# Long cross-attention by pairs of heads: scores of two heads on 64-row groups of TensorE, keys made per pair

## The reference

```python
q_hk = (hidden_q @ Wq.T).reshape(Bv, Sv, H, K)             # 256 queries, 16 heads of 128
q_big = jnp.einsum('bshk,hkq->bshq', q_hk, w_kc_q)         # 384 per head
q_big = _apply_rope(q_big, ...)
kv_r = _apply_rope(kv_c, ...)                              # 4096 x 128, one for all heads
q_r = jnp.einsum('bshq,hqr->bhsr', q_big, W_qr)            # rank 64
k_r = jnp.einsum('bld,hdr->bhlr', kv_r, W_kr)              # rank 64, per head
scores = jnp.einsum('bhsr,bhlr->bhsl', q_r, k_r)
attn = jax.nn.softmax(scores, axis=-1)
ctx_c = jnp.einsum('bhsl,bld->bhsd', attn, kv_r)
ctx_lat = jnp.einsum('bhsd,hkd->bhsk', ctx_c, w_kc_kv)
return ctx_lat.transpose(...).reshape(...) @ Wo.T          # layer ffn: |w| row max / 127, round, clip
```

## Time and profile before

| | us |
|---|---|
| median of 3 runs (range) | 1131.75 (1131.22 to 1132.66) |
| the profiled execution: its time | 1130.86 |
| its span, first to last instruction | 1129.2 |

### The profile page before, as it was taken

The page is one execution under the profiler, slowest core; times in us unless marked ns, Lnnn a source line. Parts: engine busy times, 40 slices in busy tenths (PEclk is TensorE's granted clock), DMA queues, the critical chain, the costliest instruction groups (busy, mean ns, idle before and its releaser), DMA issues.

```text
span 1129.2 us, 19389 instructions
## 1 busy us (share of the span) xinstructions
PE 1066.1 (94%) x6663; PEld 862.3 (76%) x6663; DVE 760.1 (67%) x1314; ACT 544.7 (48%) x1075; POOL 334.2 (30%) x232
## 2 busy tenths in 40 slices
PE   7989999999998998999999999999999999899995
PEld 5545889999976665888888888888898889677742
DVE  3656466556636666878888878888877887464545
ACT  3344354454423221666556566666566667343422
POOL 6810243444333000023333213333311333404411
PEclk9999899999999999999999999999999999999998
DMA  9450167655503334112111232212222211223010
GB/s 281 94 222 1 42 225 256 219 201 216 182 25 118 109 103 163 59 30 41 32 35 17 40 40 40 35 35 29 23 40 40 40 31 40 24 76 154 1 61 19
DMA packets 70510, 97.07 MB, mean 86 GB/s; under 512 B 35361, under 2 KB 52929, under 8 KB 69314
## 3 DMA queue, kind: packets, MB, share of 16 engines
q1 hardware_dynamic: 70466, 96.50, 30.2%
HBM read 91.58 MB, written 4.90 MB: 85 GB/s over the span
## 4 chain that ended last, share of the span: by engine, by line
PE 73%; DVE 17%; issue 5%; ACT 3%; DMA 1%; POOL 1%; DVEq 0%; SPq 0%; ACTq 0%; POOLq 0%
PE PS L1362 11%; PE PS L1471 11%; PE PS L1491 10%; PE PS L1481 7%; PE PS L1381 5%; DVE qsL L1024 3%; DVE pL L1050 3%; DVE scores L1030 3%; PE PS L1420 2%; PE PS L1439 2%; PE PS L1429 2%; PE PS L1210 2%; PE PS L1549 2%; PE PS L1508 1%; PE PS L1632 1%
## 5 line engine op out<-in xcount | busy, mean ns | idle before, releaser
L1030 DVE TENSOR_SCALAR_CACHE_REDUCE scores<-PS 128x512 f32<-128x512 f32 x256 | 173.9, 689 | 87.8 <-PE PS L1471 87.0
L750 ACT ACTIVATE scores<-scores,nmX 128x512 f32<-128x512 f32 x256 | 181.9, 714 | 52.8 <-DVE nmX L1034 52.4
L768 ACT ACTIVATE pH<-PS 128x1024 fp32r<-128x1024 f32 x128 | 131.0, 1023 | 152.9 <-PE PS L1481 152.9
L550 POOL TENSOR_TENSOR wrow<-wrow,winv 88x1024 f32<-88x1024 f32 x16 | 30.3, 1892 | 466.8 <-DVE winv L1070 466.8
L1050 DVE TENSOR_TENSOR pL<-PS,pH 128x1024 fp32r<-128x1024 f32 x128 | 156.2, 1220 | 7.5 <-ACT pH L768 7.5
L1481 PE MATMUL PS<-ident,scores 128*128 128x128 f32 x1024 | 136.4, 274 | 17.9 <-ACT scores L750 16.1
L1481 PEld LDWEIGHTS PS<-ident,scores 128*128 128x128 f32 x1024 | 115.9, 141 | 44.5 <-issue 34.0
L1491 PE MATMUL PS<-pH,kvH 128*128 128x256 f32 x512 | 146.5, 286 | 0.3
L1491 PE MATMUL PS<-pH,kvL 128*128 128x256 f32 x512 | 144.7, 283 | 0.0
L1491 PE MATMUL PS<-pL,kvH 128*128 128x256 f32 x512 | 144.4, 282 | 0.0
L1471 PE MATMUL PS<-kvTH,qsH 128*128 128x512 f32 x256 | 111.2, 434 | 2.0 <-DVE qsL L1024 1.5
(11 more groups left out here) (305 smaller groups left out, 2298.0 us busy)
## 6 DMA issues: line engine op xcount, KB each, us to landing
rawG<-in_wg SPq DMA_DIRECT2D x16, 768.0 KB, 5.7
rawU<-in_wu SPq DMA_DIRECT2D x16, 768.0 KB, 7.2
rawD<-in_wd SPq DMA_DIRECT2D x16, 768.0 KB, 6.3
wrow<-in_w SPq DMA_DIRECT2D x16, 352.0 KB
win<-in_win SPq DMA_DIRECT2D x1, 4640.0 KB, 17.5
wblk<-blocks SPq DMA_DIRECT2D x4, 1056.0 KB, 8.1
wb<-w_rows SPq DMA_DIRECT2D x32, 128.0 KB, 3.3
wqX<-in_wqX SPq DMA_DIRECT2D x16, 256.0 KB, 2.6
```

The lines of the kernel that those rows point to most:

```text
L750: act.activation(at, at, ACT.Exp, bias=nmX[:, b, q:q + 1], accum_out=csum[:, b, q, c:c + 1]).then_inc(exp_done, 1)
L768: act.activation(pH[:, c % 2], PS[:, 2 + 2 * (c % 2):4 + 2 * (c % 2), :].rearrange("p k (h t) -> p (k h) t", t=T), ACT.Copy).then_inc(pH_r ...
L1030: dve.tensor_scalar(sp_[:, q, c * CH:(c + 1) * CH], PS[:, q, :], 1.0, None, ALU.mult, ALU.max, accum_out=cmax[:, q, c:c + 1]).then_inc(sX_ ...
```

## The change

Heads go in pairs p; 16 slots s (or j) per pair take the place of 8 chunks per head.

- `p4` is gone. Instead `keys(p, c)` makes the keys of both heads of a pair, 64 rows for the one and 64 for the other: three matmuls 128x512 for each of 8 chunks of each pair, into bank 7; ACT copies `keyH`, DVE makes `keyL`.
- `scores(p, s)` makes chunk s // 2 and query half s % 2 for both heads: three steps of two matmuls, on rows 0 to 63 for head 0 (bank 0), on rows 64 to 127 for head 1 (bank 1). It waits until both heads' banks of the slot before are evicted (`sX_out`, 2 per slot).
- `turn(p, j)` and `weigh(p, j)` do head j % 2, chunk j // 2.
- `p3(m)` makes two heads' ranks in one group, side by side in 64-column groups.
- DVE evicts head 0's scores, makes `pL`, evicts head 1's scores; then `add_out`, `low_keys` or `row_max`.
- `qsL` and the new `wkrL` move from DVE to POOL. `keyH`, `keyL` lie where `kvr` lay, so ACT waits for `kvL_ready` ahead of the first `qh`.
- Weight rows go in 15 jobs of 256 or 128 whole rows in place of 16 of 120; `load_rows` of a job waits for `wint_ready` of the job before, and DVE's first `row_max` of it for `wrow_in`. The last layer's strided patterns become plain ones; `win` is loaded during the last pair. The loops are written out.

```diff
+            for p in range(XP):
+                sp.wait_ge(wint_ready, 2 * p + 1)
+                if p + 1 < XP:
+                    load_rows(2 * p + 1)
+                store_rows(2 * p)
...
+                if p:
+                    sp.wait_ge(oX_ps, 4 * p)
+                    load_out(p)
+                if p + 1 < XP:
+                    sp.wait_ge(wint_ready, 2 * p + 2)
+                    load_rows(2 * p + 2)
+                    store_rows(2 * p + 1)
...
+            def low_parts(p):
+                pool.wait_ge(wkrH_ready, p + 1)
+                pool.tensor_tensor(wkrL[:, p % 2], wkr[:, p % 2], wkrH[:, p % 2].bitcast(F32), ALU.subtract).then_inc(wkrL_ready, 1)
+                pool.wait_ge(qsH_ready, p + 1)
+                pool.tensor_tensor(qsL[:, p % 2], qr[:, p], qsH[:, p % 2].bitcast(F32), ALU.subtract).then_inc(qsL_ready, 1)
...
+            for p in range(2):
+                low_parts(p)
+            pool.wait_ge(qr_ready, XP)
+            for n in range(JOBS):
+                round_rows(n)
+                if n % 2 == 0 and n // 2 + 2 < XP:
+                    low_parts(n // 2 + 2)
...
+            high_parts(0)
+            high_parts(1)
+            act.wait_ge(kvL_ready, 1)
...
+            def scores_out(p, s, heads=range(2)):
+
+                c, q = s // 2, s % 2
+                dve.wait_ge(sX_ps, p * SLOTS + s + 1)
+                for h in heads:
+                    dve.tensor_scalar(sp_[:, h, q, c * CH:(c + 1) * CH], PS[:, h, :], 1.0, None, ALU.mult, ALU.max,
+                                      accum_out=cmax[:, h, q, c:c + 1]).then_inc(sX_out, 1)
+                    if c == NCH - 1:
+                        dve.wait_ge(sX_out, 2 * (p * SLOTS + s) + h + 1)
...
+            for p in range(XP):
+                for j in range(SLOTS):
+                    if j and p + 1 < XP:
+                        scores_out(p + 1, j - 1, (0,))
+                    dve.wait_ge(pH_ready, SLOTS * p + j + 1)
+                    dve.tensor_tensor(pL[:, j % 2], PS[:, 2 + 2 * (j % 2):4 + 2 * (j % 2), :].rearrange("p k (h t) -> p (k h) t", t=T),
+                                      pH[:, j % 2].bitcast(F32), ALU.subtract).then_inc(pL_ready, 1)
+                    if j and p + 1 < XP:
+                        scores_out(p + 1, j - 1, (1,))
+                    if p and j in (4, 6, 8, 10):
+                        add_out(p - 1, (j - 4) // 4, (j - 4) // 2 % 2, 7)
+                    if j % 2 and j + 1 < SLOTS and p + 1 < XP:
+                        low_keys(p + 1, (j + 1) // 2)
+                    if j == SLOTS - 2 and p + 2 < XP:
+                        low_keys(p + 2, 0)
+                    if p + 1 < XP and j in (0, 2):
+                        row_max(2 * p + 1, j // 2)
+                    if p + 1 < XP and j in (12, 14):
+                        row_max(2 * p + 2, (j - 12) // 2)
+                    if j == SLOTS - 1 and p + 1 < XP:
+                        scores_out(p + 1, SLOTS - 1)
+                dve.wait_ge(exp_done, 2 * SLOTS * (p + 1))
+                dve.tensor_reduce(recX[:, p % 2], csum[:, p % 2], AX.X, ALU.add).then_inc(csum_done, 1)
...
+            def keys(p, c):
+
+                if c == 0:
+                    pe.wait_ge(wkrL_ready, p + 1)
+                for j, (w, v) in enumerate(((wkrH, kvTH), (wkrH, kvTL), (wkrL, kvTH))):
+                    mm = pe.matmul(PS[:, 7, :], w[:, p % 2, :], v[:, c * CH:(c + 1) * CH], start=(j == 0), stop=(j == 2))
+                mm.then_inc(key_ps, 1)
...
+            def scores(p, s):
+
+                c, q = s // 2, s % 2
+                if s == 0:
+                    pe.wait_ge(qsL_ready, p + 1)
+                if q == 0:
+                    pe.wait_ge(keyL_ready, p * NCH + c + 1)
+                wait(pe, sX_out, 2 * (p * SLOTS + s))
+                for j, (w, v) in enumerate(((qsH, keyH), (qsH, keyL), (qsL, keyH))):
+                    for h in range(2):
+                        rank = slice(XR * h, XR * h + XR)
+                        mm = pe.matmul(PS[:, h, :], w[rank, p % 2, q * P:(q + 1) * P], v[rank, c * CH:(c + 1) * CH], start=(j == 0), stop=(j == 2),
+                                       skip_group_check=True)
+                mm.then_inc(sX_ps, 1)
...
+            for p in range(XP):
+                more = p + 1 < XP
+                for j in range(SLOTS):
+                    turn(p, j)
+                    if j and more:
+                        scores(p + 1, j - 1)
+                    if p and j == 2:
...
+                        keys(p + 1, (j + 1) // 2)
+                    if j:
+                        weigh(p, j - 1)
+                    if j == SLOTS - 2 and p + 2 < XP:
+                        pe.wait_ge(keyL_ready, (p + 2) * NCH)
+                        keys(p + 2, 0)
+                    if j == SLOTS - 1 and more:
+                        scores(p + 1, SLOTS - 1)
+                weigh(p, SLOTS - 1)
+            values(XP - 1)
```

More of the change, by code:

```diff
@@ new lines, in _ @@
+            act.wait_ge(kvL_ready, 1)
+            for n in range(XH):
+                act.wait_ge(p1_done, n + 1)
+                wait(act, p2_done, n - 1)
+                act.activation(qh[:, n % 2], PS[:, n % 2, 0:T], ACT.Copy).then_inc(qh_ready, 1)
+                if n % 2 and n >= 5:
+                    ranks_out((n - 5) // 2)
+                    if (n - 5) // 2 < 2:
+                        high_query((n - 5) // 2)
+                if n % 2 == 0 and n:
+                    high_keys(0, n // 2 - 1)
@@ L785, in _ @@
+            contexts_out(XP - 1)
+            values_out(XP - 1)
             for t in range(NT):
@@ L1078, in _, with low_keys @@
-            step(dve.memset(wmax[:], 0.0))
-            for b in range(2):
-                stage_query(b, b)
-            for c in range(NCH):
-                scores_out(0, c, 0)
-            pairs(dve, dve_scores)
-            add_out(XH - 1, 1, 0)
-            add_out(XH - 1, 1, 1)
+                wait(dve, p3_done, (n - 4) // 2 + 1)
+                dve.tensor_tensor(qb[:, n % 4], qm1[:], qm2[:], ALU.add).then_inc(qb_ready, 1)
+            def low_keys(p, c):
+                dve.wait_ge(keyH_ready, p * NCH + c + 1)
+                at = slice(c * CH, (c + 1) * CH)
+                dve.tensor_tensor(keyL[:, at], PS[:, 7, :], keyH[:, at].bitcast(F32), ALU.subtract).then_inc(keyL_ready, 1)
@@ L1528, in _ @@
-            pe.wait_ge(kvL_ready, 1)
-            for c in range(NCH):
-                scores(0, 0, c)
-            turn(0, 0)
-            pairs(pe, pe_scores)
-            values(XH - 1, 1, XH // 2)
-            for q in range(NT):
-                head_out(XH - 1, 1, q)
-            stay_awake(14, 0)
+            for n in range(XH):
+                if n + 1 < XH:
+                    p1(n + 1, (n + 1) // 2, (n + 1) % 2)
+                if n % 2 and n >= 3:
+                    p3((n - 3) // 2)
+                p2(n, n // 2, n % 2)
+                if n % 2:
+                    wait(pe, keyL_ready, n // 2)
+                    keys(0, n // 2)
@@ new lines, in weigh @@
+            def weigh(p, j):
+                h, c = j % 2, j // 2
+                pe.wait_ge(pL_ready, SLOTS * p + j + 1)
+                if c == 0:
+                    wait(pe, cT_ready, p)
+                for m in range(4):
+                    for k, (w, v) in enumerate(((kvH, pH), (kvH, pL), (kvL, pH))):
+                        mm = pe.matmul(PS[:, 6, h * T:(h + 1) * T], w[:, 4 * c + m, :], v[:, j % 2, m, :],
+                                       start=(j == 0 and m == 0 and k == 0), stop=(c == NCH - 1 and m == 3 and k == 2), skip_group_check=True)
+                mm.then_inc(v_done, 1)
@@ new lines, in values, with head_out @@
+            def values(p):
+                pe.wait_ge(wo2_in, (p + 1) * 32)
+                pe.wait_ge(cT_ready, p + 1)
+                for h in range(2):
+                    mm = pe.matmul(PS[:, 7, h * T:(h + 1) * T], kcv[:, h, :], cT[:, h, :], start=True, stop=True)
+                mm.then_inc(vX_ps, 1)
+            def head_out(p, h, q, bank):
+                pe.matmul(PS[:, bank, :], vT[:, h, q * P:(q + 1) * P], woX[:, h, :], start=True, stop=True).then_inc(oX_ps, 1)
+            for s in range(SLOTS):
+                scores(0, s)
+                if s == 1:
+                    wait(pe, keyL_ready, NCH)
+                    keys(1, 0)
```

495 lines of the change are left out of this document (224 added, 271 removed).

## The result

The changed kernel takes 1156.1 us (median of 4 runs, 1151.4 to 1159.5) against 1131.6 for the kernel before: a ratio of 1.0215, 95% interval 1.0183 to 1.0248. It is slower by 24.5 us, inside the forecast's own range (1134 to 1165) and 9.4 above its number. The profiled execution took 1156.57 us, 25.7 more than that of before.

What follows compares the result with a forecast made beforehand. The prediction took PE's sequence to bound the kernel. Projections -13.5, first scores +32.7, seven pairs -22, last pair +21.2 and last layer -3.5 gave +14.9 on 1130.86, a median of 1146.7 us; range 1106 to 1172, forecast's own 1134 to 1165.

Steps and rivals of the forecast that it cites:

- What bounds it, and the slot: PE's sequence bounds the heads; a paired slot takes 3.38 us, 4.08 with keys, including 0.39 for shape changes.
- The first rival: Changes of weight shape in the score slots cost nothing: 1108 us, faster; chance 16%.
- the fourth: Rival: score steps of two heads do not overlap with fp32r, +0.70 on 128 slots, 1236 us; chance 2%.
- the 0.216: PE's time in us per 256 columns of a matmul, taken from L1420's row of the earlier profile.
- The pairs: Seven pairs in the overlapped loop take 473 us against 495.1: -22, with 67.3 per pair.
- The row job of the seam is just covered: Between pairs, weight rows land 9.4 us after DVE's reciprocal and DVE reaches its wait after 8.9.
- The ring: DVE's evict, `pL`, evict takes 3.5 us between scores; it binds at the seam, and two plain slots lose 0.1 each.
- the third rival: DVE's ring decides every slot, at 4.3 to 4.4 us, a pair 70.4: +22, 1169; chance 12%.
- First scores: The first pair's scores, standing alone, take 48.6 us against 15.9: +33, at 3.05 a slot.
- Last pair, projections, last layer: Last pair with its tail +21.2 us, projections ahead of the scores -13.5, last layer's products -3.5.
- without `kvL` it would be -21: In the projections, without ACT's wait for POOL's `kvL`, the gain would be -21 us, not -13.5.
- The second rival: Clock holds in first scores (-9), first row load in time (-8), seams lose 1, not 3.3 (-16): 1114 us; 18%.

Runs made afterwards that it cites:

- e3_all_rows: `e1_rows_late` with score matmuls on all 128 rows for each head, so no shape change and nothing side by side; 1171.6 us.
- e4_same_rows: `e1_rows_late` with both matmuls of a score step on rows 0 to 63, so shape changes stay but nothing runs side by side; 1228.5 us.
- e1_rows_late: The changed kernel with the first and second row maximum of the seam's job in slots 4 and 6 of a pair, not 0 and 2; 1133.3 us.
- e2_pl_after: `e1_rows_late` with both of DVE's score evictions ahead of the low part of the probabilities, not one before and one behind; 1122.9 us.
- e7_awake: `e2_pl_after` with five small matmuls on PE after each of the first pair's score slots but the last; 1111.1 us.
- e12_kvl_parts: `e2_pl_after` plus two bank sets for first scores, ACT's later `kvL` wait, `wkrL` of two pairs ahead of `kvL`, and `kvL` in eight instructions; 1085.8 us.

## Why the prediction was right, and where it was off

**What bounds it, and the slot.** Right to 0.01 us: 3.37 (plain) and 4.07 (with keys) measured for 3.38 and 4.08. `e3_all_rows` and `e4_same_rows` measured the two parts by themselves, 0.68 for side by side and 0.39 for the shape. The first rival (shape for nothing) and the fourth (no overlap) are out. Two readings were loose without harm. That nothing is lost between blocks of one shape is so but for the first score matmul behind the transposes, which takes 0.31 before the change as well; and the 0.216 follows from L1420's row only when the 0.10 that its first record loses to the change of shape is taken off.

**The pairs.** This is the step that was off: "The row job of the seam is just covered". The forecast had the rows land 9.4 after DVE's reciprocal and DVE at its wait after 8.9. In pair 1 the reciprocal starts at 542.41, DVE comes free at 550.9, 8.5 later, and the rows are there at 552.4, 10.0 later; POOL ended after 6.1 and the load took 3.9, not the 3.3 taken. The 0.5 in each pair that this reckoning itself had was set at nothing, and behind it stands a serial chain: wait, row maximum (0.6), then the eviction. Only the first pair's wait was in the sum, with +8; the experiment shows 22 for all seven, 8 of them through the lower clock around the waits, which the forecast named for the first pair alone. The rest of the step held in its sum: without the +8 the seven pairs were forecast at 465, and `e1_rows_late`, without the wait, takes 465.3. That close a match is partly luck. Its pairs in the middle take 66.6, forecast 67.3, with the seam's 3.3 of waits measured as 1.6 (slots 15 and 0), 0.9 (slot 2) and 0.2 (slot 13); but its first pair takes 66.1, forecast 63, since its odd slots take 4.30 by DVE's ring and it starts at the low clock.

**The ring.** The forecast saw it bind only at the seam and in the two plain slots. It did, in slot 13, and in the odd slots of the first pair besides (4.30 for 4.08); the third rival (in each slot) is out. It did not say that another order avoids it: `e2_pl_after` gets 1.8 per pair of it back.

**First scores.** +30.3 for +32.7: full clock held for three slots, then 3.1, as in the earlier trace rows. That a slot waits for both evictions is what made it long: with a second pair of banks it is 24.5 less, and the clock then stays at 0.95.

**Last pair, projections, last layer.** +22.6 for +21.2, -11.6 for -13.5, -4.6 for -3.5: sizes within 2. The first `p2` started at 356.05 for a forecast of 354.9, and the projections took 70.0 for 69.3. But "without `kvL` it would be -21" was too much for that wait alone: behind it stand POOL's `wkrL` and DVE's `qb`, and three edits together bring the start of the scores to 417.9, which is -19.8.

**State-space layer.** Not in the sum: 3.0 of its 3.5 lie in some 80 matmuls that took 20.5 at a granted clock of 0.85 before and take 17.5 at 1.00 now. Why the clock is up there was not tried. So the number was 10.7 off between the two traces because 14.4 too little for the pairs met 3.7, on balance, of other errors the other way, this one and the first scores above all.

**The second rival** (fixed parts cheaper) named as its conditions that the clock holds, that the first row load lands in time, and that the seams lose 1. None came true by itself, and each could be had by an edit: 8.6 (`e7_awake`), 22.8 (`e1_rows_late`), 10.4 (`e2_pl_after`).

So the change is slower because a loop over pairs doubles what stands alone at both ends (+53 measured), while a pair in the middle, even without the row wait, takes 66.6 where two heads took 66.0; with the better order it takes 64.7. With the ends and the order mended, `e12_kvl_parts` is 3.9% faster than the kernel before.
